# Queries and keys as two float32r parts, and two heads side by side in the rows of the array

## The reference

```
L0: x = ln(x + mha(x, x, window 64, ALiBi bias)); x = ln(x + mha(x, ctx)); x = ln(x + gelu(x@w1+b1)@w2+b2)
L1: x = ln(x + mha(x, x, causal));                x = ln(x + mha(x, ctx)); x = ln(x + gelu(x@W1+b1)@W2+b2)
L2: x = x + mha(ln(x), ln(ctx));                  x = x + silu(x@W1+b1)@W2+b2
L3: x = ln(x + mha(x, ctx))
mha: q, k, v = projections, 16 heads of 16 features; softmax(q k^T * scale + bias, masked) v, then @ wo + bo
```

## Time and profile before

| | |
|---|---|
| median of 3 executions | 3558.36 us (3557.86 to 3558.53) |
| profiled execution, span | 3565.0 us |
| PE busy | 3446.8 us (97%) |
| PEld busy | 1657.1 us (46%) |
| DVE busy | 2572.8 us (72%) |
| ACT busy | 1935.0 us (54%) |
| POOL busy | 1143.4 us (32%) |
| DMA | 280.64 MB, queue q1 24.0% of 16 engines |

### The profile page before, as it was taken

How to read it: one execution, slowest core, us unless ns; L and a number is a source line. 1 busy time by engine, 2 the same in 40 slices (tenths; PEclk the granted TensorE clock), 3 DMA queues, 4 the chain that set the end, 5 groups by cost and what they waited for, 6 DMA issues and landing times.

```text
span 3565.0 us, 53384 instructions
## 1 busy us (share of the span) xinstructions
PE 3446.8 (97%) x18672; PEld 1657.1 (46%) x18932; DVE 2572.8 (72%) x6523; ACT 1935.0 (54%) x2375; POOL 1143.4 (32%) x1049
## 2 busy tenths in 40 slices
PE   8899999999999999999999999999999999999998
PEld 5545544433454554443354455444335445445333
DVE  5766887756886588766778668777577956976667
ACT  2454565555555456555555545555564654655555
POOL 4322432222532242222253223222235322322222
PEclk9999999999999999999999999999999999999999
DMA  6311321223321231122332122112133312211211
GB/s 213 123 46 55 118 67 54 86 60 93 103 78 43 81 114 46 54 87 60 93 123 74 47 93 82 47 53 87 60 109 110 96 54 81 66 46 63 75 54 55
DMA packets 284317, 280.64 MB, mean 79 GB/s; under 512 B 49858, under 2 KB 275266, under 8 KB 280066
## 3 DMA queue, kind: packets, MB, share of 16 engines
q1 hardware_dynamic: 258324, 274.84, 24.0%
q10 hardware_dynamic: 25728, 2.36, 0.6%
HBM read 195.84 MB, written 81.26 MB: 78 GB/s over the span
## 4 chain that ended last, share of the span: by engine, by line
PE 83%; DVE 11%; issue 2%; ACT 2%; DMA 1%; SPq 1%; POOL 0%; another core or an unknown queue 0%; ACTq 0%; DVEq 0%
PE pv L718 14%; PE st L693 14%; PE mx L670 13%; PE mx L768 10%; PE mx L645 10%; PE st L731 9%; DVE row_max L911 5%; PE mx L742 4%; PE st L654 4%; PE mx L765 2%; PE st L778 2%; DVE mx L914 2%; ACT probs L829 1%; DVE turned L934 1%; DMA rows_of_max_dram<-max_rows 1%
## 5 line engine op out<-in xcount | busy, mean ns | idle before, releaser
L829 ACT ACTIVATE probs<-st 128x1024 f32<-128x1024 f32 (+1 forms) x1344 | 1266.6, 977 | 696.4 <-PE st L693 419.1
L911 DVE TENSOR_REDUCE row_max<-mx 128x1 bf16<-128x512 f32 x2048 | 1283.8, 684 | 216.3 <-PE mx L670 121.0
L1021 POOL TENSOR_TENSOR qm<-q_high,own_rows 128x512 bf16<-128x512 bf16 x768 | 797.3, 1044 | 1583.5 <-PE mx L670 1183.6
L670 PE MATMUL mx<-k_high,qm 128*128 128x512 bf16 (+4 forms) x2812 | 815.2, 342 | 44.7 <-DVE row_max L911 18.2
L693 PE MATMUL st<-q_packed,k_packed 97*128 97x512 bf16 (+2 forms) x3072 | 816.0, 346 | 27.3 <-DMA q_packed<-q_parts_dram 9.9
L718 PE MATMUL pv<-probs,va 128*32 128x512 f32 (+2 forms) x6144 | 701.8, 532 | 12.0 <-ACT probs L829 7.1
L670 PEld LDWEIGHTS mx<-k_high,qm 128*128 128x128 bf16 x3072 | 284.3, 98 | 604.0 <-DVE row_max L911 211.1
L914 DVE CUSTOM_DVE_ANT_0 mx<-mx,tab 128x192 f32<-128x192 f32 (+4 forms) x1024 | 400.9, 444 | 132.4 <-PE mx L670 118.7
L693 PEld LDWEIGHTS st<-q_packed,k_packed 97*128 97x128 bf16 (+1 forms) x3072 | 279.6, 98 | 435.0 <-ACT probs L829 149.8
L731 PE MATMUL st<-xT,w1s 128*128 128x512 f32 x768 | 342.9, 592 | 0.0
L957 DVE TENSOR_TENSOR y<-mx,row 128x256 f32<-128x256 f32 x224 | 94.8, 423 | 299.9 <-PE mx L768 297.2
(11 more groups left out here) (88 smaller groups left out, 3141.5 us busy)
## 6 DMA issues: line engine op xcount, KB each, us to landing
k_packed<-k_parts_dram SPq DMA_DIRECT2D x576, 128.0 KB, 2.7
q_packed<-q_parts_dram SPq DMA_DIRECT2D x576, 128.0 KB, 2.7
q_parts_dram<-q_low SPq DMA_DIRECT2D x96, 256.0 KB, 2.2
k_parts_dram<-k_low SPq DMA_DIRECT2D x96, 256.0 KB, 2.5
q_parts_dram<-q_high SPq DMA_DIRECT2D x48, 256.0 KB, 2.1
k_parts_dram<-k_high SPq DMA_DIRECT2D x48, 256.0 KB, 2.3
w1s<-w_dram SPq DMA_DIRECT2D x12, 1024.0 KB, 5.1
w2s<-w_dram SPq DMA_DIRECT2D x12, 1024.0 KB, 7.6
```

The lines of the kernel that those rows point to most:

```text
L670: mm = pe.matmul(bank[:, 0:k1 - k0], qm[:, h % RING, i * P:(i + 1) * P], high["k"][s][:, t, k0:k1], start=True, stop=True)
L829: act.activation(dst[:, :, 0:w], held["scores", b, a, n, e][:, :, 0:w], ACT.Exp, scale=ATT_SCALE[a]) \
L911: ins = dve.tensor_reduce(top, scores, AX_X, ALU.max, negate=True)
L1021: pool.tensor_tensor(qm[:, h % RING], high["q"][s][:, h // HT], own_rows[:, h % HT:h % HT + 1].to_broadcast([P, TOK]), ALU.mult) \
```

## The change

- q and k become two float32r parts, `high` (ACT) and `low` (DVE, straight from PSUM); the stage `middle` is gone, and with it `rest`. Three products of parts make 48 rows, with maximum and slopes 49 or 58. Two heads stand in one buffer, the even one in rows 0 to 63, the odd one in rows 64 to 127.
- `scores`: matmuls of an even and an odd head follow each other, each over its 64 rows and into its own bank. The mask is one matmul for each bank, over all 128 rows.
- `max`: one stage for a pair of heads. Features are permuted (`feature`) so that even heads lie in the upper 64 rows and odd ones in the lower; one POOL mask serves two heads (384, not 768), two matmuls of 64 rows fill two banks, and one `tensor_reduce` of both gives two columns. Masks and biases of maxima are now added on PE, with `eye`; the custom operation is gone.
- PSUM: one ring of three pairs for everything (`ring_pair`), and two banks for `pv`.
- `project` and `project_v` are cut in two stages, `rows` drains two rows of tokens at once, the maxima are float32 and come back by two DMAs per group, `sums` is a single buffer, the constant rows go through DRAM at the start.
- All MERGE strings are new. In the old order PE changes 1462 times between matmuls over the whole array and `values` in its column groups; in the new one, with row halves as a third way, 3604 times.

```diff
-HML = "hml"
-PART = {"k": {"h": (0, 1, 2), "m": (3, 4), "l": (5,)}, "q": {"h": (1, 3, 5), "m": (2, 4), "l": (0,)}}
-MAXROW = 6 * HD
+HL = "hl"
+PART = {"q": {"h": (0, 1), "l": (2,)}, "k": {"h": (0, 2), "l": (1,)}}
+PARTS = 3
+MAXROW = PARTS * HD
+def feature(h):
+    return h // HT * HT + h % 2 * (HT // 2) + h % HT // 2
...
-        high = {m: [sb(f"{m}_high{s}", [P, KT, TOK], BF16) for s in range(SLOTS)] for m in "qk"}
+        high = {m: [sb(f"{m}_high{s}", [P, KT, TOK], F32R) for s in range(SLOTS)] for m in "qk"}
-        packed = {m: sb(f"{m}_packed", [P, H, TOK], BF16) for m in "qk"}
+        packed = {m: sb(f"{m}_packed", [P, NP, TOK], F32R) for m in "qk"}
-        st = stack.enter_context(nc.psum_tensor("st", [P, 2, 2, TOK], F32))
-        pv = stack.enter_context(nc.psum_tensor("pv", [P, TOK], F32))
-        mx = stack.enter_context(nc.psum_tensor("mx", [P, 3, TOK], F32))
+        st = stack.enter_context(nc.psum_tensor("st", [P, RING, 2, TOK], F32))
+        pv = stack.enter_context(nc.psum_tensor("pv", [P, 2, TOK], F32))
...
+        def in_rows(h, count, first=0):
+            return slice(h % 2 * HALF_ROWS + first, h % 2 * HALF_ROWS + first + count)
...
+            def ring_pair(signal, name):
+                n = len(drains)
+                drains.append(signal.past(name))
+                if n >= RING:
+                    pe.wait_ge(*drains[n - RING])
+                return st[:, n % RING]
...
-                    bank = held["max", b, a, h, i] = mx_bank()
-                    mm = pe.matmul(bank[:, 0:k1 - k0], qm[:, h % RING, i * P:(i + 1) * P], high["k"][s][:, t, k0:k1],
-                                   start=True, stop=True)
+                    pair = held["max", b, a, p, i] = ring_pair(mx_drained, ("max", b, a, p, i))
+                    for odd in range(2):
+                        block = in_rows(odd, HALF_ROWS)
+                        mm = pe.matmul(pair[:, odd, 0:k1 - k0], qm[block, p % MASKS, i * P:(i + 1) * P],
+                                       high["k"][s][block, t, k0:k1], start=True, stop=(k_kind == FULL))
+                    if k_kind == CAUSAL:
+                        for odd in range(2):
+                            mm = pe.matmul(pair[:, odd, i * P:(i + 1) * P], tb("eye"), tb("hide_qk"), start=False, stop=True)
+                    if k_kind == WINDOW:
+                        for odd in range(2):
+                            bias_of = tb("wbias_qk")[:, 0:(2 * p + odd + 1) * WCOL]
+                            mm = pe.matmul(pair[:, odd, 0:k1 - k0], tb("eye"), bias_of[:, bias_of.shape[1] - (k1 - k0):bias_of.shape[1]],
+                                           start=False, stop=True)
...
+                        contracted = in_rows(h, MAXROW + 1 + (SLOPES if k_kind == WINDOW else 0))
+                        mm = pe.matmul(flat[:, c:c + w], packed["k"][contracted, h // 2, k * P:(k + 1) * P],
+                                       packed["q"][contracted, h // 2, q0:q1], start=(not shared or j < 2), stop=(k_kind == FULL))
+                    if k_kind != FULL:
+                        hide = tb("hide_kq") if k_kind == CAUSAL else tb("whide_kq")[:, 0:w]
+                        heads_of_bank = 2 if shared else 1
+                        hidden = hide.shape[1]
+                        for bank in range(2):
+                            to = pair[:, bank, 0:heads_of_bank * w].rearrange("p (h n) -> p h n", n=w)[:, :, 0:hidden]
+                            mm = pe.matmul(to, tb("eye"), hide.unsqueeze(1).to_broadcast([P, heads_of_bank, hidden]),
+                                           start=False, stop=True)
...
-                        ins = dve.tensor_tensor_reduce(scores, scores, hide[:, hide.shape[1] - (k1 - k0):hide.shape[1]], -1.0, 1e30,
-                                                       ALU.add, ALU.min, top)
+                    dve.tensor_reduce(row_max[s][:, c:c + TT + 1:TT], held["max", b, a, p, i][:, :, 0:k1 - k0], AX_X, ALU.max,
+                                      negate=True).then_inc(*mx_drained.mark(("max", b, a, p, i)))
...
-        "11": "011100111101000021100111121012112220202101002211101011210101122220000210112121212221101201101001"
-           "0110102011011211000212222220222222020222022022200220220000222002222202222022200",
+        "11": "101012000011201222102200022200121121022210001221221210000021022010020120001022020202021220221022"
+           "2022202020220222002200000022022200022002",
```

More of the change, by code:

```diff
@@ L7 @@
 F32 = mybir.dt.float32
+F32R = mybir.dt.float32r
 BF16 = mybir.dt.bfloat16
@@ L110 @@
 LOOPS = [(SLOTS * i + s, a) for i in range(B // SLOTS) for a in range(6) for s in range(SLOTS)]
+STRANDS = ["steps", "maxima", "between", "context", "folds"]
 LOOP_NO = {ba: j for j, ba in enumerate(LOOPS)}
@@ L122, in max_column, with keys, maxima_stages @@
     return h // GRP * BLK + h % GRP * TT + i
[L125 to L129, removed]
-        for i in range(TT):
[L131 to L135, removed]
+def keys(kind, i):
+    return (max(0, i * P - WIN) if kind == WINDOW else 0), TOK if kind == FULL else (i + 1) * P
+def maxima_stages(b, a, pairs):
+    for p in pairs:
+        if p and p + MASKS - 1 < NP:
+            yield "mask", b, a, p + MASKS - 1
+        for i in range(TT):
+            yield "max", b, a, p, i
+        if p % 2:
+            yield "max_rows", b, a, p // 2
+        if p % 2 == 0 and p or p == NP - 1:
+            yield "max_back", b, a, (p - 1) // 2
 def step_stages(b, a):
@@ L191, in prefetched, with project_stages, value_stages @@
     return a == 0 and b >= SLOTS
+def project_stages(b, a, m):
+    for t in range(KT):
+        yield "project", b, a, m, t
+def value_stages(b, a):
+    for half in range(2):
+        yield "project_v", b, a, half
 def start_stages(b, a):
-    yield "project", b, a, "q"
+    yield from project_stages(b, a, "q")
+    for p in range(MASKS):
+        yield "mask", b, a, p
     if own(a):
[L198 to L204, removed]
+        yield from project_stages(b, a, "k")
+        yield from value_stages(b, a)
     yield "load", b, a, 0
@@ L214, in context_stages @@
         yield from norm_stages(b, "ctx")
-    yield "project", b, a, "k"
-    yield "middle", b, a, "k"
-    yield "project_v", b, a
+    yield from project_stages(b, a, "k")
+    yield from value_stages(b, a)
     if a == 5:
@@ L239, in streams @@
     b, a = LOOPS[j]
-    steps, maxima = list(step_stages(b, a)), list(maxima_stages(b, a, range(AHEAD, H)))
+    steps, maxima = list(step_stages(b, a)), list(maxima_stages(b, a, range(AHEAD, NP)))
     between, context = [], []
@@ L612, in _ @@
                         pe.wait_ge(folds_in, 3 * 16)
-                    bank = held["fold", n, t] = mx_bank()
+                    pair = held["fold", n] = ring_pair(mx_drained, ("fold", n, KT - 1)) if t == 0 else held["fold", n]
+                    bank = pair[:, t]
                     for k in range(KT):
@@ new lines, in _ @@
+                    for j in range(KT):
+                        mm = pe.matmul(held["proj", b, a, m][:, t], sqw(f"{m}{a}")[:, j, t * P:(t + 1) * P], src[:, j, :],
+                                       start=(j == 0), stop=(j == KT - 1))
+                    mm.then_inc(*mx_filled.mark(("proj", b, a, m, t)))
+                elif kind == "project_v":
+                    a, half = stage[2:]
+                    if half == 0:
+                        pe.wait_ge(*keys_of(b, a))
+                        held["v", b, a] = ring_pair(st_drained, ("v", b, a))
+                    pair = held["v", b, a]
+                    for i in (2 * half, 2 * half + 1):
@@ L773, in _ @@
                     pe.wait_ge(*row_step.past(("scale", b, tag, half)))
-                    pair = held["turn", b, tag, half] = st_pair()
+                    pair = held["turn", b, tag, half] = ring_pair(st_drained, ("turn", b, tag, half))
                     for j in range(KT):
```

390 lines of the change are left out of this document (178 added, 212 removed).

## The result

The changed kernel takes 3790.86 us (3787.08 to 3798.79, 4 runs) against 3558.45 us on the same chip: a ratio of 1.0656, interval 1.0641 to 1.0671. It is 232 us slower, where 236 us less were forecast.

A forecast was written before the change was run, and what follows sets the result against it. PE's instruction stream, busy 97% of 3565.0 us, was taken as the bound. −550 + 70 + 214 − 50 + 75 + 5 = −236 gave 3329, less 6.6: 3322 us; forecast band 3200 to 3440, range 3170 to 3560.

The forecast's parts named there:

- Maxima and scores: PE's maxima and scores matmuls: float32r streams in one pass and both row halves run together, −550 us.
- Rival C: Pairs of maxima and scores: halves do not run together, or float32r takes two passes; slower, 3872 us, chance 0.10.
- point of decision: Pairs of 512 columns in maxima and scores: above 0.31 us a pair the changed kernel becomes slower.
- Masks: Causal and window maxima masked on PE by 1024 matmuls with `eye`: +70 us; masks in the scores 0.
- Switches: PE changing between row halves, column groups and whole array: 2142 more changes at 0.10 us, +214 us.
- DVE, ACT, POOL: Other engines' work falls, DVE to about 2176 us, ACT by 101; by itself 0, with less PE waiting −50 us.
- shorter masked maxima: PE's weight loads wait less for masked maxima on DVE: −50 us of the 72 us waited.
- The ring: Three PSUM pairs for everything, in program order: PE waits in full-attention steps, a third of 220 us unfilled, +75 us.
- Rival A: The PSUM ring binds, all 220 us unfilled and no relief from masked maxima: 3517 us, chance 0.12.
- no clock is left to win: PE's granted clock is 1.00 behind the start, 2.4 GHz; no term in us was given.
- Loads: DMA loads and sends hidden, 0; constant rows through DRAM in the first 100 us, +5 us.
- D: Rival on PE's changes of array division: each costs a full drain, 0.16 us; +198 us, 3520 us, chance 0.05.

The follow-up runs named there:

- cut versions: Changed kernel and the one before, each with reduces and exponentials cut to 32 columns so PE hardly waits: 3562.72 and 3500.36 us.
- rates: Matmuls only, in a row, no kernel: 512-column float32r pairs 0.230 us, bf16 pairs 0.216; a change of division 0.105, a float32r load behind it 0.11 more.
- short_both: Changed kernel with every reduce of the maxima and every exponential cut to 32 columns of each bank: 3562.72 us, ratio 1.0014.
- before_short_both: Kernel before the change with reduces, masked custom operations and exponentials cut to 32 columns: 3500.36 us, ratio 0.9834.
- no_masks: Changed kernel without its mask matmuls in window and causal attention, in maxima and scores: 3719.31 us, ratio 1.0456.
- masks_on_dve: Changed kernel in its own order, only the masks of window and causal maxima moved back to DVE: 3790.53 us, ratio 1.0640.
- bf16_halves: Changed kernel with parts and maxima in bf16 in place of float32r, full reduces and exponentials: 3615.31 us, ratio 1.0167.

## Why the prediction was wrong

The loss of 232 us is, by the cut versions, 62 us of stream (3563 against 3500) and 170 us of waits (3791 − 3563 = 228, against 3558 − 3500 = 58). The division is rough, since the cut versions keep waits of their own. The forecast had −266 us of stream and +30 of the rest: it missed the stream by 328 us and the waits by 140.

1. *Maxima and scores, −550.* The mechanism was right: one pass, both halves together, 0.230 us a pair (rates). Only the price was 0.014 us a pair too low: 2544 × 0.014 = 36 us. Rival C, both in turn or two passes, is out, though its point of decision, 0.31 us a pair, was passed: pairs of the changed kernel cost 0.34 us behind a change.
2. *Masks, +70.* Not far off: in the trace of the changed kernel two mask matmuls of 192 columns lie 0.093 us apart and two of 128 0.066, against 0.085 and 0.058 here, 8 us over 1024.
3. *Switches, +214.* This is the step that failed, and by its term: the change itself costs 0.105 us, as taken from `values`, but I read it from entries whose weights come quickly: 32 columns, or bf16. The load of 128 four-byte columns shows behind a change with the same 0.11 us at which it holds the narrow matmuls of rates. There are 1651 entries into row halves, and 374 into float32 over the whole array where the kernel before has 87: 1651 × 0.11 and 287 × 0.104 us are some 212 us for which the prediction had nothing; so this term is 437 us (225 for 2142 changes at 0.105, 212 for loads) and not 214. For the type alone the same prices give 182, with the 36 of point 1 and some 27 of narrow pairs 245; measured are 221. The prediction held the number that would have shown it, 190 against 98 ns, and used it only for the question whether two loads go side by side. By the Trainium skill ("TensorE: Matmul & The Clock Gate", LDWEIGHTS) a load takes its columns at 1.2 GHz; by that, as an estimate, 107 ns for 128. The time that shows agrees: the first float32 record behind a pair takes 0.533 us in rates, 0.104 above its 0.429. The load's own record is longer, 190 ns. Together −550 + 36 + 70 + 8 + 225 (2142 × 0.105) + 212 + 27 = +28, measured +62; 34 us are not attributed, and PE is idle 40 us longer in short_both than in before_short_both.
4. *DVE, ACT, POOL.* ACT falls by 66 us and not 101. DVE has 2420 us and not 2176: a reduce of 1024 columns lasts 1.218 us as worked out, but the next often starts later than the 1.13 us that were reckoned (1298.6 us for 1088). The saving of 252 us on the masked maxima was also too large by the sum it started from: 401 + 148 = 549 us, where the custom operations and the reads of the accumulator overlap and keep DVE busy for 422 us together. The −50 for shorter masked maxima can't be told from the next point; the sum of both is measured.
5. *The ring, +75.* With point 4, +25 were forecast and +170 measured. A third of the hand-made gap unfilled was a guess, and it was the guess with the least behind it. Rival A, with all of the ring's 220 us and no relief from masked maxima, had +220 (195 above the forecast), and so came nearest in this term. That the three pairs are waited for is shown by the cut versions (DVE 82, both 228 us) and by the waits of PE's loads in the changed kernel, which answer to the earlier trace rows (us in total, times, longest):

```profile
PEld st L725 <- DVE row_max L943: 181.2, 241, 1.7
...
PEld st L725 <- ACT probs L866: 131.1, 199, 1.7
...
PEld st L697 <- ACT probs L866: 113.1, 180, 8.0
PEld st L697 <- DVE row_max L943: 109.0, 188, 1.7
```

In the kernel before the maxima's loads waited 283 us for DVE, and the scores' for ACT:

```profile
PEld st L693 <- ACT probs L829: 149.8, 225, 0.8
```

Now DVE ends 290 us of the waits and ACT 244: a score tile waits for a reduce and a maximum for an exponential, since both draw from one ring, and what rose is ACT's part, and the longest waits (0.9 to 1.7 us for DVE). How much of it the number of pairs makes, apart from the order, is not shown: eight banks hold no fourth pair beside `pv`, and no other number was tried. The forecast also had no term for the clock: "no clock is left to win" was right, and it could be lost. From 57 to 167 us at the lower level, at most half of the difference, 55 us, if PE streams all that time; that is part of the 170.
6. *Loads.* The first 100 us have PE busy 81.7 us and 79.4 before; nothing was lost there.

The range ended at 3560, where A and D were each let in alone. They were no alternatives: 198 and 195 us on top of the forecast make 3715, and D's mechanism (a full drain for each change) was wrong in kind, but near in size, by luck: its 198 us stand for changes of 0.16 us, and what was missing were 212 us of shown loads.

## What to carry to other kernels

Price a change of the array's division by what follows it: 0.105 us if bf16 weights come next, and 0.10 to 0.11 more for 128 four-byte columns, which doubles it. Halving the columns of a matmul pays only where several such matmuls follow one another in the same division: here one pair saves 0.20 us and an entry and exit cost 0.32, and there are 3072 pairs, wide and narrow, in 1651 stays. When PE's stream is shortened in front of engines with 1 us per buffer and three buffers for all, look at the idle time and the granted clock together before counting the gain: of 162 us of busy time that no_masks took off PE the kernel kept 71, and of 47 that masks_on_dve took off, none.

## What the runs showed of the hardware that I had not expected

- Float32r weight loads of 128 columns hold narrow matmuls at 0.11 us each, single or as a pair of row halves (128 and 192 columns alike); bf16 pairs of 192 take 0.08 us.
- The two matmuls of a pair of row halves share one slot of 0.230 us. Behind a change they start 2 to 5 ns apart, in the unbroken row of float32r pairs of rates mostly 36 to 38 ns.
- With the same instructions in another order (after_replan) the mean granted clock was 0.962 and not 0.978: 290 us at 1.2 GHz instead of 167, with PE busy 93% of the span; no_masks and masks_on_dve, at 91 and 92%, had 0.954 and 0.956. But bf16_halves, also at 91%, had 0.987, so the busy share doesn't decide it.
